# Edge scores computed inside the first gather pass and a bitonic sort spread over the third, on one NeuronCore

## The reference, cut to what matters

```python
def _L0(h, w, src, dst, W, b):
    m = h[src] * w
    agg = segment_sum(m, dst); cnt = segment_sum(ones, dst)
    return relu(concatenate([h, agg / maximum(cnt, 1)]) @ W.T + b)

def _L1(nodes, edges, r, s, W, W_edge, a, ...):          # plus self loops
    Wn = einsum('hfi,ni->nhf', W, nodes); We = einsum('hfi,ei->ehf', W_edge, e)
    msg = (Wn[s]*a_s).sum + (Wn[r]*a_r).sum + (We*a_e).sum    # We*a_e: the edge scores
    alpha = softmax over each receiver of leaky_relu(msg)
    out = segment_sum(alpha * Wn[s], r)                      # then elu, layer norm

def _L2(feat, weight, src, dst, etypes):
    return segment_sum(feat[src] @ weight[etypes], dst)

def _L3(inputs, edge_index, W, a):                       # row, col = src, dst
    e = exp(leaky(score[row] + score[col]))              # two heads
    return mean over heads of segment_sum(e * inputs[col], row) / segment_sum(e, row)

x = norm(x + _L0(x, edge_weight1, src, dst)); x = norm(x + _L1(x, edge_attr_16, dst, src))
x = norm(x + _L2(x, weight, src, dst, edge_type_16)); x = norm(x + _L3(x, [src, dst]))
```

## Time and profile before

| | |
|---|---|
| median of 3 runs | 19102.6 us (19095.28 to 19102.89) |
| the profiled execution's own time | 19103.92 us |
| its span in the profile | 19101.2 us |
| first pass, first gather to last | 164.5 to 4213.4 us |
| block with edge scores and sort | 4428.1 to 5469.9 us |
| third pass, first gather to last | 10601.8 to 14648.5 us |
| POOL busy over the span | 12531.0 us (66%) |
| DVE busy over the span | 9230.2 us (48%) |

### The profile page before, as it was taken

How to read it: one execution, slowest core, us unless ns; L and a number is a source line. 1 busy time by engine, 2 the same in 40 slices (tenths; PEclk the granted TensorE clock), 3 DMA queues, 4 the chain that set the end, 5 groups by cost and what they waited for, 6 DMA issues and landing times. The chain is left out here.

```text
span 19101.2 us, 250826 instructions
## 1 busy us (share of the span) xinstructions
PE 8282.0 (43%) x37230; PEld 7312.8 (38%) x37231; DVE 9230.2 (48%) x26702; ACT 4224.7 (22%) x18246; POOL 12531.0 (66%) x13216
## 2 busy tenths in 40 slices
PE   2333333336025555555527433333333344444443
PEld 2333333335015555555522333333333344444443
DVE  4333333338957777777752333333333544444444
ACT  1222222221002222222211000000000344444443
POOL 7777777760017777777740677777775677777775
PEclk9999999999999999999999999999999755555555
DMA  1111111111023333333322111111110222222222
GB/s 47 26 26 26 26 26 26 26 29 63 15 64 86 85 85 85 85 85 84 85 69 90 46 26 26 26 26 26 26 26 18 55 53 53 53 53 53 53 53 46
DMA packets 713373, 937.18 MB, mean 49 GB/s; under 512 B 303241, under 2 KB 324509, under 8 KB 710871
## 3 DMA queue, kind: packets, MB, share of 16 engines
q0 software_dynamic: 423856, 454.56, 11.9%
q1 hardware_dynamic: 289448, 481.91, 7.9%
HBM read 723.02 MB, written 206.21 MB: 49 GB/s over the span
## 5 line engine op out<-in xcount | busy, mean ns | idle before, releaser
L416 POOL DMA_INDIRECT l_rows<-t_d,l_idx_st x3232 | 3063.1, 948 | 1705.1 <-issue 920.3
L475 DVE TENSOR_TENSOR acc<-acc,l_ps 128x65 f32 (+1 forms) x6464 | 1439.4, 223 | 5258.4 <-DVE acc L475 3592.4
L1042 POOL DMA_INDIRECT gat_rows<-t_d,gat_idx_st x3232 | 3067.9, 949 | 1007.9 <-issue 933.2
L416 POOL DMA_INDIRECT l_rows<-in_x,l_idx_st x3232 | 3065.2, 948 | 994.6 <-issue 984.3
L1714 POOL DMA_INDIRECT p_rows<-x_d,p_idx_st x3232 | 3063.4, 948 | 993.2 <-issue 956.3
L431 PE MATMUL l_ps<-l_rows,l_oh 128*128 128x64 f32 x6464 | 1482.9, 424 | 2586.1 <-DVE acc L475 1680.0
L431 PE MATMUL l_ps<-l_msg,l_oh 128*128 128x65 f32 x6464 | 1482.7, 421 | 2579.3 <-DVE acc L475 2319.1
L431 PEld LDWEIGHTS l_ps<-l_rows,l_oh 128*128 128x128 f32 x6464 | 1409.1, 330 | 2661.2 <-DVE acc L475 2586.6
L431 PEld LDWEIGHTS l_ps<-l_msg,l_oh 128*128 128x128 f32 x6464 | 1408.7, 330 | 2653.2 <-DVE acc L475 2589.3
L1146 PE MATMUL gat_ps<-gat_msg,gat_oh 128*128 128x72 f32 x6464 | 1488.4, 425 | 1059.7 <-DVE gat_msg L1206 1059.7
L1146 PEld LDWEIGHTS gat_ps<-gat_msg,gat_oh 128*128 128x128 f32 x6464 | 1409.1, 330 | 1176.3 <-DVE gat_tot L1226 1143.1
(11 more groups left out here) (289 smaller groups left out, 11806.4 us busy)
## 6 DMA issues: line engine op xcount, KB each, us to landing
cur_d<-gat_cur SPq DMA_DIRECT2D x404, 288.0 KB
gat_keyrow<-keyb_d SPq DMA_DIRECT2D x404, 256.0 KB
p_keyrow<-keyb_d SPq DMA_DIRECT2D x404, 256.0 KB, 3.2
l_rows<-in_x,l_idx_st POOLq DMA_INDIRECT x3232, 2.4
gat_rows<-t_d,gat_idx_st POOLq DMA_INDIRECT x3232
l_rows<-t_d,l_idx_st POOLq DMA_INDIRECT x3232, 2.4
p_rows<-x_d,p_idx_st POOLq DMA_INDIRECT x3232
t_d<-t_tab SPq DMA_DIRECT2D x98, 512.0 KB, 2.6
```

The source lines that it names most:

```text
L416: pool.indirect_dma_start(rows[:, r, s, :], None, table, bass.IndirectOffsetOnAxis(idx_st[:, r, s:s + 1], 0)).then_inc(s_rows[r], 16)
L475: dve.tensor_tensor(there, there, part, ALU.add).then_inc(s_acc, 1)
L1042: pool.indirect_dma_start(rows[:, r, s, :], None, m.t1_d, bass.IndirectOffsetOnAxis(idx_st[:, r, s:s + 1], 0)).then_inc(s_rows[r], 16)
```

## The change

`sum_pass` and `edge_scores_and_sort` are gone. Two functions stand in their place. `first_pass` is the first gather pass with the edge scores inside it. After every fourth group (a turn), in turns 0 to 53, PE makes the products of the chunk before and the transposes of this turn's chunk, and ACT makes the two copies; `scores` in each engine's code does that. The scores are kept in two buffers of one chunk and stored to DRAM a chunk at a time by SP. DVE's part in it is the small set-up before the loop.

`second_pass` (so named in the code; in the order of the program it is the third gather pass) has the sort inside it. DVE's generator `sort` yields after each stage, and `loop` calls it once after each of the first 224 groups, which are written out one by one and not in a hardware loop. A `quarters` stage takes three groups: two with nothing, while SP's DMAs run, and one with its three instructions. Of each exchange stage, ACT first copies the upper half of every pair to a PSUM buffer `high` (2048 columns); DVE's minimum and maximum then read one input from PSUM and one from SBUF. The window numbers of a group are loaded with one call, ahead of the wait for PE.

```diff
+        def passes(eng, group, scores):
+            def turn(i, b):
+                for r in range(RINGS):
+                    group(i * RINGS + r, r)
+                scores(i, b)
...
+            def scores(i, b):                                   # ACT
+                if among(i, 1):
+                    act.wait_ge(s_turned, i)
+                    act.copy(eaT[:, 1 - b], pt[:, :, 0:EP]).then_inc(s_eaT, 1)
+                if among(i, 2):
+                    act.wait_ge(s_emm, i - 1)
+                    act.copy(se[:, b], po[0:EP, 0:CH * E8 * HEADS]).then_inc(s_se, 1)
...
+            def scores(i, b):                                   # PE
+                if among(i, 1):
+                    pe.wait_ge(s_eaT, i)
+                    for c in range(CH):
+                        ins = pe.matmul(po[...], eaT[:, 1 - b, c, :], bd[...])
+                if among(i, 0):
+                    for c in range(CH):
+                        ins = pe.transpose(pt[:, c, 0:EP], ea[:, b, c, :], ...)
...
+        def loop(eng, body, beside):                            # second_pass, ACT and DVE
+            for n in range(SORTING):
+                body(n, n % RINGS)
+                next(beside, None)
+            with eng.Fori(SORTING // RINGS, TURNS - 1) as i:
...
+            def halves():                                       # ACT
+                        act.wait_ge(s_sort, at)
+                        x = pairs_of(keys[0], j, k)
+                            act.copy(high[:]..., x[:, :, 1]).then_inc(s_high, 1)
...
+            def add(n, r):                                      # DVE
+                _, js = nc.values_load_multi_w_load_instructions(m.winrow[0:1, bass.ds(n * U, U)], ...)
+                dve.wait_ge(s_mm, n + 1)
...
+                        dve.wait_ge(s_high, made)
+                            dve.tensor_tensor(y[:, :, 0], h, x[:, :, 0], ALU.min)
+                            so(dve.tensor_tensor(y[:, :, 1], h, x[:, :, 0], ALU.max))
-                    dve.tensor_tensor(y[:, :, 0], x[:, :, 0], x[:, :, 1], ALU.min)
-                    so(dve.tensor_tensor(y[:, :, 1], x[:, :, 0], x[:, :, 1], ALU.max))
...
-                    sum_pass(nc, m, "l0", x, None, True, tabs=(...))
+                    first_pass(nc, m, x, edge_attr, W1, W1e, a1)
-            edge_scores_and_sort(nc, m, edge_attr, W1, W1e, a1, src, dst)
-                sum_pass(nc, m, "l2", ..., m.rel_d, False)
+                second_pass(nc, m, ..., m.rel_d, src, dst)
```

More of the change, by code:

```diff
@@ new lines, in _, with body @@
+        @block.gpsimd
+        def _(pool):
+            def body(n, r, first, last):
+                pool.wait_ge(s_staged, n + 1)
+                if not first:
+                    pool.wait_ge(s_msg, n - RINGS + 1)
+                alone(pool)
+                for s in range(U):
+                    pool.indirect_dma_start(rows[:, r, s, :], None, table,
+                                            bass.IndirectOffsetOnAxis(idx_st[:, r, s:s + 1], 0)).then_inc(s_rows[r], 16)
+            turns(pool, body)
@@ L668, in _ @@
[L668 to L689 removed]
+            pe.wait_ge(s_ones, 2)
@@ L691, in _, with body @@
+            passes(pe, group, scores)
         @block.vector
         def _(dve):
+            def add(n, r):
+                dve.wait_ge(s_mm, n + 1)
+                for s in range(U):
+                    add_to_window(dve, m, ps[:, r % 2, s, 0:WD], n * U + s, WD, s_acc)
+            def body(n, r, first, last):
+                dve.wait_ge(s_staged, n + 1)
+                if after(first, 2, r):
+                    dve.wait_ge(s_mm, n - 1)
+                onehots(dve, m, oh[:, r % 2], key_st[:, r], s_oh)
+                if after(first, 1, r):
+                    add(n - 1, (r - 1) % RINGS)
@@ new lines, in _, with body @@
+        @block.gpsimd
+        def _(pool):
+            def body(n, r, first, last):
+                pool.wait_ge(s_staged, n + 1)
+                if not first:
+                    pool.wait_ge(s_mm, n - RINGS + 1)
+                alone(pool)
+                for s in range(U):
+                    pool.indirect_dma_start(rows[:, r, s, :], None, table,
+                                            bass.IndirectOffsetOnAxis(idx_st[:, r, s:s + 1], 0)).then_inc(s_rows[r], 16)
+            turns(pool, body)
@@ new lines, in _, with body @@
+        @block.tensor
+        def _(pe):
+            def body(n, r, first, last):
+                pe.wait_ge(s_oh, n + 1)
+                pe.wait_ge(s_rows[r], rows_in(n, r))
+                if after(first, 2, r):
+                    pe.wait_ge(s_acc, (n - 1) * U)
+                for s in range(U):
+                    ins = pe.matmul(ps[:, r % 2, s, 0:D], oh[:, r % 2, s, :], rows[:, r, s, :], start=True, stop=True)
+                ins.then_inc(s_mm, 1)
+            turns(pe, body)
+        @block.vector
```

562 lines of the change are left out of this document (298 added, 264 removed).

## The result

The changed kernel takes 18118.6 us (median of 4 runs, 18115.1 to 18121.3) against 19100.4 us of the kernel before on the same chip (4 runs): a ratio of 0.9486, 95% interval 0.947 to 0.9503, or 982 us less. Forecast were 18215 us and 887 us less. The change pays as said, and 97 us more than said. The profiled execution took 18121.3 us, its span is 18119.5.

The account below looks back on a forecast made before the run. Each pass was taken as bound by POOL's gathers, with about 2 us of slack in DVE's chain per group. 19103.9 - 1041.8 + 155 = 18217 us profiled, forecast 18215; range 18090 to 18460, to hold 8 in 10.

Parts of the forecast that it names:

- What goes: The block with edge scores and sort, between `nodes_0` and the next block, disappears with nothing covering it: 1041.8 us removed.
- The first pass: PE's 5.5 us of added score work per turn fits in 6.3 us free: 0 added.
- The third pass: With sort stages, DVE's group takes 10.97 us against POOL's 10.02, so the pass gets 155 us longer.
- 3.59 us to the first add: DVE's group, third pass: 0.55 us from first one-hot to the load, then 3.04 us to the first add.
- The rest of the sum: DVE's group, third pass: adds 2.78 us, long exchange stage 4.50, wait for the stage's semaphore some 0.1.
- PSUM as an input: DVE's minimum with one input in PSUM takes 2.30 us at 2048 columns against 2.291 from SBUF: no cost.
- ACT's copy: Third pass: ACT's copy of 2048 columns to PSUM takes 2 us, hidden within 6.4 us.
- Rival 1: Third pass: a sort group needs 10.02 us or less, POOL stays the bound, nothing is added: 18062 us, chance 0.08.
- Rival 3: DVE's sort instructions and POOL's gathers shut each other out: 720 us more, 18935; chance of full lock-out 0.05.
- The signs named ahead: Third pass: gathers pausing about 1 us per group, DVE's group 11 us; prediction wrong if gathers exceed 0.95 us.
- Rivals 2, 4, 6: Load not hidden, 18455 us (0.15); first pass longer by up to 240, 18455 (0.06); next block waits, some 18500 (0.02).
- Rival 5: Fetching the long written-out code stalls the engines, 6 us a group, 1310 us in all: 19525 us, chance 0.03.

Follow-up runs that it names:

- e_scores_moved: Kernel before, with only the edge scores moved into the first pass; the sort alone in its block, third pass as before: 19097.3 us, ratio 0.9998.
- e_sort_moved: Kernel before, with only the sort moved into the third pass; the edge scores in a block of their own: 18501.2 us, ratio 0.9687.
- e_pe6: Changed kernel, with PE making each chunk's eight edge products six times in the first pass: 18363.0 us, ratio 0.9613.
- e_wait: Changed kernel, with DVE's wait for a sort stage's end moved to just before the next stage: 18105.1 us, ratio 0.9476.
- e_copy2: Changed kernel, with ACT making one more copy of the 2048 columns ahead of each real one: 18128.8 us, ratio 0.9489.
- e_copy4: Changed kernel, with ACT making three more copies of the 2048 columns ahead of each real one: 18450.8 us, ratio 0.966.
- e_sides_act: Changed kernel, with the moved wait of `e_wait` and the eight `sides` stages made by ACT instead of DVE: 18084.8 us, ratio 0.9467.

## Why the prediction was right, point by point

- **What goes**, 1041.8 us: measured 1043.1 (5469.89 - 4426.78), 1.3 of it from work before the block that ended that much earlier. The gap before `table_1` is 0.53 us, as said. That nothing covered this stretch is shown by `e_scores_moved` and `e_sort_moved`.
- **The first pass**, 0: measured -2.4. Right, and `e_pe6` gives the cover.
- **The third pass**, +155: measured +59.4. This is nearly the whole miss of 97 us, and it is the sum of two errors of opposite sign. DVE's group is 10.26 us, not 10.97: 0.71 x 218 = 155 us, so with it the prediction's own sum adds about nothing. And the longer gathers, put at nothing, cost about 50 (`e_wait`). Had the gathers not grown longer, the same forecast would have been some 150 us too high: that it came within 97 is in part luck. The mechanism was half right: DVE is behind through most of the sort, by 0.24 us a group, but most of the 59.4 us is POOL's own. The step of the sum that failed most is its first, 3.59 us to the first add. I let the load begin 0.55 us behind the one-hots, as in the earlier trace rows. In the changed kernel:

```profile
L859 DVEq TENSOR_LOAD <-winrow x1: 595/595/595, 10704.9 to 10704.9; - x1
```

  It starts with the one-hots (10704.86), takes 0.60 us, and eight register operations of the same line follow it, 0.28 us apart; so the first add comes 3.06 us after the one-hots. As I read it, the sequencer had the one-hots ready while it waited for the sort stage and sent them off at once; 0.55 was read where nothing held them back.
- The rest of the sum: adds 2.77 for 2.78; the stage starts 0.08 before the last add's end (10710.61 and 10710.69) and its link costs 0.03, where I put 0.1; the stage 4.48 for 4.50. With 3.06 that makes 3.06 + 2.77 - 0.08 + 4.48 + 0.03 = 10.26.
- **PSUM as an input** costs nothing: 2.28 us for 2.29 before. The rule of the Trainium skill (VectorE: DVE Perf Modes, section on the TRN2 errata) that I weighed, 120 cycles fixed against 58, would have made it about 2.36, an estimate from that page; the trace does not agree.
- **ACT's copy**, 2 us and hidden: 1.87 us, hidden, with room for twice as much and not for four times (`e_copy2`, `e_copy4`).
- **Rival 1** (POOL stays the bound, 18062) was nearer the truth than its 0.08. DVE's group is 0.24 us above POOL's (0.37 in the stages of four instructions), not 1. `e_wait` takes that away and shows that POOL does not then reach 18062.
- **Rival 3** (lock-out): right that with one input in PSUM the exchange stages hold nothing up, and near in the size of the rest, "40 us at most"; wrong in "where it has slack". In the changed kernel the gathers are 43.6 us longer than before, nearly all of it in 18 gathers of 2.1 to 6.6 us, beside the `sides` and `quarters` stages and a few instructions like them. With DVE's group so close to POOL's there is little slack; in `e_wait` all 50 us are on the path. How the changed kernel's 59.4 splits between DVE's longer group and this, no run tells exactly: without the first 50.0 remain, so the first decides over some 10 only.
- **The signs named ahead**: two came out against the forecast's mechanism. The gathers' mean is 961 ns, over the 950 that was to show the prediction wrong, where it was 948 before. And the gathers do not pause 1 us a group: in the whole pass they are idle 15.3 us more, and wait for PE 25.6 us where it was 64.3. One-hots to one-hots is 10.26 us and not 11. The others held: first pass, barrier, ACT's copy, the minimum from PSUM.
- **Rivals 2, 4, 6** did not occur. **Rival 5** (long code) occurs in small; see below.

Best of all is `e_sides_act`, 18084.8 us, 1017 us less than the kernel before on its chip.

## What to carry to other kernels

A block costs its longest chain. Before work is moved out of one, find how long the second chain is, since that is what remains. Beside a pass that is bound by gathers on GpSimd, the DVE work tried here was nearly free as long as it fitted into the group's time, had at most one input in SBUF and was not a wide `TENSOR_SCALAR`; an idle ACT can bring one input to PSUM, or do that stage itself. A wait placed right behind an instruction stops the sequencer's own work too; placed before the first reader it lets the load of the window numbers run on beside it, worth 9.4 us of the pass here.

## What the runs showed of the hardware

- A gather that starts while DVE runs an instruction of 1024 columns or more with two SBUF inputs, or a `TENSOR_SCALAR` of 4096 columns, is held at its start: in the stages shown it ends 0.81 to 0.83 us after DVE's does. A `TENSOR_SCALAR` also holds one that is under way: the first gather below had begun 0.43 us before, and ended 0.11 after. The longest, 6.6 us, starts beside the second of the three instructions of a `quarters` stage and ends 0.12 us after the third. DVE is not slowed.

```profile
11366.56 2.89 POOL L838 DMA_INDIRECT l_rows<-t_d,l_idx_st  x1 [0.30 <-issue]
11366.99 2.35 DVE L925 TENSOR_SCALAR l_kc<-l_kc,l_low 128x4096 f32<-128x4096 f32 x1
11369.37 4.48 DVE L926 SCALAR_TENSOR_TENSOR l_kc<-l_ka,l_low,l_kc 128x4096 f32<-128x4096 f32 x1
11369.76 6.60 POOL L838 DMA_INDIRECT l_rows<-t_d,l_idx_st  x1 [0.30 <-issue]
11373.89 2.35 DVE L927 TENSOR_SCALAR l_kc<-l_kc,l_low 128x4096 f32<-128x4096 f32 x1
```

- With 4096 columns on ACT, or with one input in PSUM, there is no such effect beyond some hundredths of a microsecond a group: in `e_sides_act` the 11 gathers of over 1.3 us make 28.4 of the 29.7 us.
- The second group above has an idle time of 1.73 us before its adds where 1.37 is usual. Such gaps of about 0.35 us in DVE's sequencer recur in the written-out part: the trace shows 22 between 10310 and 11800 us, all 128 of DVE's rows apart or a multiple of that, so about every third group. They cost about 0.1 us a group, where rival 5 had feared 6. The instruction queue moved 136 packets of 8 KB (1.11 MB) where it moved 52. In the trace such a packet starts 0.65 to 0.97 us after 21 of the 22 gaps, and the one before had landed over 20 us earlier in 20 of them. So a gap goes with a packet being asked for, and is not a wait for one to land. What the sequencer does in it stays open. The Trainium skill (Runtime: NRT & Kernel Launch, section on instruction fetch mechanics) counts 512 instructions to 32 KiB, which makes 128 to such a packet, an estimate from that page, and holds that the cost of going from one block of instructions to the next is mostly hidden. As to the first the trace agrees; as to the second, the packets' own time is hidden here and 0.35 us a packet is not, where DVE has nothing else to do.
